# Feed-forward activations split into fp16 pairs two tiles at a time, with eight pair buffers

## The reference

```python
def ffn(x, ...):                                    # 8 experts, top 4 of them, and a shared one
    gate = einsum('bsd,ed->bse', x, Wg) + routing_bias
    weights = softmax over the top 4 of gate
    swiglu = (sigmoid(h) * h * v) @ w3.T            # h = x @ w1.T, v = x @ w2.T, 341 hidden units
    return swiglu_shared(x) + sum_e weights[e] * swiglu_e(x)

x = x + 0.5 * ffn(layernorm(x))
x = x + attention(layernorm(x))                     # 16 heads of 64, causal, softmax
x = x + 0.5 * ffn(layernorm(x))                     # the same weights again
```

## Time and profile before

| | |
|---|---|
| median of 3 runs | 685.14 us (684.83 to 685.91) |
| span of the profiled execution, first to last instruction | 683.0 us |
| TensorE busy | 646.1 us, 95% |
| VectorE busy | 609.6 us, 89% |
| ScalarE busy | 572.8 us, 84% |
| GpSimd busy | 495.7 us, 73% |
| mean granted TensorE clock | 0.995 |

### The profile page before, as it was taken

The page is one execution under the profiler, slowest core; times in us unless marked ns, Lnnn a source line. Parts: engine busy times, 40 slices in busy tenths (PEclk is TensorE's granted clock), DMA queues, the critical chain, the costliest instruction groups (busy, mean ns, idle before and its releaser), DMA issues.

```text
span 683.0 us, 20985 instructions
## 1 busy us (share of the span) xinstructions
PE 646.1 (95%) x7846; PEld 414.1 (61%) x7846; DVE 609.6 (89%) x1701; ACT 572.8 (84%) x1110; POOL 495.7 (73%) x589
## 2 busy tenths in 40 slices
PE   5798989999999998999899999999999999999997
PEld 3465755465567565666566566665666567666665
DVE  4899799999998999899889999989999888789887
ACT  6789977898999888899978999997999997565654
POOL 3244775688899687788967889895789898566555
PEclk9999999999999999999999999999999999999999
DMA  7800000278799366588844788683678797100000
GB/s 205 258 1 1 1 2 1 54 111 148 120 129 154 57 104 120 100 140 123 145 75 79 114 140 141 125 137 56 102 125 134 144 144 110 33 1 18 17 2 16
DMA packets 226489, 62.97 MB, mean 92 GB/s; under 512 B 213202, under 2 KB 225620, under 8 KB 226388
## 3 DMA queue, kind: packets, MB, share of 16 engines
q1 hardware_dynamic: 226388, 61.64, 52.4%
HBM read 7.87 MB, written 1.05 MB: 13 GB/s over the span
## 4 chain that ended last, share of the span: by engine, by line
PE 45%; DVE 23%; ACT 16%; issue 9%; POOL 5%; DMA 1%; SPq 0%; ACTq 0%; DVEq 0%; POOLq 0%
PE bank L1068 13%; PE bank L1070 12%; PE bank L1069 12%; ACT probs L1424 6%; DVE probs L1710 4%; DVE glu L1619 3%; DVE xs L1649 3%; ACT glu L1386 3%; PE bank L1238 3%; DVE glu L1624 3%; POOL paired L1035 2%; ACT gluh L1407 2%; PE bank L1201 2%; POOL glul L1031 1%; ACT paired L1432 1%
## 5 line engine op out<-in xcount | busy, mean ns | idle before, releaser
L1031 POOL TENSOR_TENSOR glul<-glu,gluh 128x512 f16<-128x512 f32 x191 | 221.3, 1161 | 98.4 <-ACT gluh L1407 97.9
L1035 POOL TENSOR_TENSOR paired<-probs,paired 128x512 f16<-128x512 f32 x160 | 185.4, 1161 | 27.4 <-ACT paired L1432 24.5
L1386 ACT ACTIVATE glu<-bank,tanh_scale 128x512 f32<-128x512 f32 x167 | 113.3, 678 | 49.1 <-PE bank L1070 48.5
L1619 DVE SCALAR_TENSOR_TENSOR glu<-glu,bank 128x512 f32<-128x512 f32 x167 | 113.7, 681 | 24.8 <-ACT glu L1386 24.4
L1424 ACT ACTIVATE probs<-probs,exp_bias 128x128 f32<-128x128 f32 (+3 forms) x256 | 131.6, 551 | 3.6 <-POOL exp_bias L1043 3.5
L1710 DVE CUSTOM_DVE_ANT_0 probs<-bank,causal,score_scale 128x128 f32<-128x128 f32 (+3 forms) x256 | 128.0, 545 | 6.2 <-POOL paired L1035 5.0
L1068 PE MATMUL bank<-w3h,gluh 128*128 128x128 f16 x708 | 127.4, 220 | 5.9 <-POOL glul L1031 4.9
L1070 PE MATMUL bank<-w3h,glul 128*128 128x128 f16 x708 | 127.2, 220 | 0.0
L1069 PE MATMUL bank<-w3l,gluh 128*128 128x128 f16 x708 | 127.2, 220 | 0.0
L1407 ACT ACTIVATE gluh<-glu 128x512 f16<-128x512 f32 x191 | 118.5, 621 | 2.0 <-DVE glu L1624 2.0
L1624 DVE SCALAR_TENSOR_TENSOR glu<-glu,bank 128x512 f32<-128x512 f32 x167 | 114.7, 687 | 5.8
(11 more groups left out here) (236 smaller groups left out, 1619.8 us busy)
## 6 DMA issues: line engine op xcount, KB each, us to landing
pT<-paired SPq DMA_TRANSPOSE x160, 3.2
attention_raw<-in_L_attn_W_qkv SPq DMA_DIRECT2D x6, 256.0 KB, 5.3
xs<-in_L_attn_inputs SPq DMA_DIRECT2D x4, 256.0 KB, 4.7
vh<-in_L_ffn_W SPq DMA_DIRECT2D x6, 128.0 KB
pT<-in_L_ffn_W SPq DMA_DIRECT2D x6, 128.0 KB
out<-xs SPq DMA_DIRECT2D x3, 256.0 KB, 2.5
raw_more<-in_L_ffn_W SPq DMA_DIRECT2D x4, 128.0 KB
attention_raw<-in_L_attn_W_out SPq DMA_DIRECT2D x2, 256.0 KB, 6.4
```

The lines of the kernel that those rows point to most:

```text
L1031: pool.tensor_tensor(glul[pair][:, :], g[:, :], gluh[pair][:, :], ALU.subtract).then_inc(glu_low)
L1035: pool.tensor_tensor(paired[n % PAIRED][:, 1, :], probs[n % PROBS][:, :], paired[n % PAIRED][:, 0, :], ALU.subtract).then_inc(probs_low)
L1386: act.activation(g[:, :], psum[b1.bank][:, :], ACT.Tanh, scale=tanh_scale[:, j:j + 1]).then_inc(tanh_made)
L1619: v.scalar_tensor_tensor(g[:, :], g[:, :], 1.0, psum[b1.bank][:, :], ALU.add, ALU.mult).then_inc(drained[b1.bank])
```

## The change

Two neighbouring tiles are split by one instruction of 1024 columns on each engine, every second step. `glu`, `gluh` and `glul` each become one tensor with the buffers side by side, so that two neighbouring buffers can be named by one slice. SPLIT_LAG goes from 2 to 3: at the odd steps i = 3, 5, ... 25 the tiles i - 3 and i - 2 are split together. DOWN_LAG stays 4. GLU_PAIRS goes from 7 to 8, so that a pair of tiles never wraps around. The waits count splits instead of tiles. In stream 7 the tiles 20 and 21 are one split at step 22; tile 22 and the two halves of tile 23 stay as they were. So 191 splits of 512 columns become 95 of 1024 and one of 512.

```diff
-SPLIT_LAG = 2
+SPLIT_LAG = 3
...
-GLU_PAIRS = 7
+GLU_PAIRS = 8
...
-    def split_hidden(self, j, tiles):
-        t = tiles[j]
-        self.add("split_hidden", k=t["k"], g=t["g"], b2=t["b2"], pair=t["pair"], left=self.pair_left[t["pair"]])
+    def split_hidden(self, js, tiles):
+
+        of = [tiles[j] for j in js]
+        first, n = of[0], len(of)
+        assert all(t["g"] == first["g"] + i and t["pair"] == first["pair"] + i for i, t in enumerate(of))
+        self.glu_splits += 1
+        for t in of:
+            t["split"] = self.glu_left[t["g"]] = self.glu_splits
+        self.add("split_hidden", split=self.glu_splits, g=slice(first["g"], first["g"] + n), b2s=[t["b2"] for t in of],
+                 pair=slice(first["pair"], first["pair"] + n), left=max(self.pair_left[t["pair"]] or 0 for t in of))
...
-            elif SPLIT_LAG <= i < HT + SPLIT_LAG:
+                if i < HT:
+                    self.split_hidden({HT - 2: order[HT - 4:HT - 2], HT - 1: order[HT - 2:HT - 1]}[i], tiles)
+            elif SPLIT_LAG <= i < HT + SPLIT_LAG and (i - SPLIT_LAG) % 2 == 0:
                 assert self.scales_known
-                self.split_hidden(order[i - SPLIT_LAG], tiles)
+                self.split_hidden(order[i - SPLIT_LAG:i - SPLIT_LAG + 2], tiles)
...
-                    g, pair = glu[s["g"]], s["pair"]
-                    q.wait_ge(glu_high, s["k"] + 1)
-                    pool.tensor_tensor(glul[pair][:, :], g[:, :], gluh[pair][:, :], ALU.subtract).then_inc(glu_low)
+                    q.wait_ge(glu_high, s["split"])
+                    pool.tensor_tensor(glul_all[:, s["pair"], :], glu_all[:, s["g"], :], gluh_all[:, s["pair"], :],
+                                       ALU.subtract).then_inc(glu_low)
...
-                    q.wait_ge(glu_low, s["k"] + 1)
+                    q.wait_ge(glu_low, s["split"])
                     drain_of(s["w_ready"])
...
-                    b2, pair = s["b2"], s["pair"]
-                    q.wait_ge(drained[b2.bank], b2.n + b2.d)
+                    for b2 in s["b2s"]:
+                        q.wait_ge(drained[b2.bank], b2.n + b2.d)
                     if s["left"]:
                         q.wait_ge(down_done, s["left"])
-                    act.activation(gluh[pair][:, :], glu[s["g"]][:, :], ACT.Copy).then_inc(glu_high)
+                    act.activation(gluh_all[:, s["pair"], :], glu_all[:, s["g"], :], ACT.Copy).then_inc(glu_high)
```

More of the change, by code:

```diff
@@ L323, in hidden @@
         self.glu_taken += 1
-        self.add("hidden", k=k, c=c, j=j, b1=b1, b2=b2, g=g, halves=halves,
+        self.add("hidden", k=k, c=c, j=j, b1=b1, b2=b2, g=g, halves=halves, glu_left=self.glu_left[g],
                  x_ready=self.halves_ready[halves], w_ready=[u for n in OWNERS[j] for u in (self.weights_ready[n, 0], self.weights_ready[n, 1])])
@@ L333, in last_hidden @@
         banks = [(self.bank(), self.bank()) for _ in range(2)]
+        split = self.glu_splits + 1
+        self.glu_splits += 2
         self.add("last_hidden", k=k, c=c, j=j, banks=banks, g=g, halves=halves, x_ready=self.halves_ready[halves],
-                 pair=k % GLU_PAIRS, left=self.pair_left[k % GLU_PAIRS])
-        tiles[j] = {"k": k, "g": g, "b2": banks[1][1], "pair": k % GLU_PAIRS}
+                 pair=k % GLU_PAIRS, left=self.pair_left[k % GLU_PAIRS], glu_left=self.glu_left[g], split=split)
+        tiles[j] = {"k": k, "g": g, "b2": banks[1][1], "pair": k % GLU_PAIRS, "split": split}
     def native_hidden(self, j, tiles):
@@ L357, in down @@
         self.parts += 1
-        self.add("down", part=PARTS.index((j, n)), k=t["k"], pair=t["pair"], first=first, last=last, use=use,
+        self.add("down", part=PARTS.index((j, n)), k=t["k"], split=t["split"], pair=t["pair"], first=first, last=last, use=use,
                  w_ready=self.weights_ready[n, 2])
@@ L378, in down_crossed @@
             first, last = self.turn_of_part(c, n)
-            sides.append({"part": PARTS.index((j, n)), "k": tiles[j]["k"], "pair": tiles[j]["pair"], "first": first,
+            sides.append({"part": PARTS.index((j, n)), "split": tiles[j]["split"], "pair": tiles[j]["pair"], "first": first,
                           "last": last, "use": self.down_uses[n], "w_ready": self.weights_ready[n, 2]})
@@ L756, in macaron @@
         route = [sb(f"route{i}", [P, NE, NT]) for i in range(2)]
-        glu = [sb(f"glu{i}", [P, L]) for i in range(GLUS)]
-        gluh = [sb(f"gluh{i}", [P, L], F16) for i in range(GLU_PAIRS)]
-        glul = [sb(f"glul{i}", [P, L], F16) for i in range(GLU_PAIRS)]
+        glu_all = sb("glu", [P, GLUS, L])
+        gluh_all, glul_all = sb("gluh", [P, GLU_PAIRS, L], F16), sb("glul", [P, GLU_PAIRS, L], F16)
+        glu = [glu_all[:, i, :] for i in range(GLUS)]
+        gluh, glul = ([of[:, i, :] for i in range(GLU_PAIRS)] for of in (gluh_all, glul_all))
         qk = [[sb(f"{n}{i}", [P, L], F16) for n in ("qh", "ql", "kh", "kl")] for i in range(2)]
@@ L1010, in gpsimd @@
                         part = slice(h * L // 2, (h + 1) * L // 2)
-                        q.wait_ge(glu_high, s["k"] + 1 + h)
+                        q.wait_ge(glu_high, s["split"] + h)
                         pool.tensor_tensor(glul[pair][:, part], g[:, part], gluh[pair][:, part], ALU.subtract
@@ L1182, in tensor @@
                         if s["k"] == 2 * B * HT - 1 and t == NT // 2:
-                            q.wait_ge(glu_low, s["k"] + 2)
+                            q.wait_ge(glu_low, s["split"] + 1)
                         done = three_pass(psum[use.bank][:, t * D:(t + 1) * D], gluh[pair][:, rows],
@@ L1191, in tensor @@
                     for side in s["sides"]:
-                        q.wait_ge(glu_low, side["k"] + 1)
+                        q.wait_ge(glu_low, side["split"])
                         drain_of(side["w_ready"])
@@ L1378, in scalar @@
                     q.wait_ge(filled[b1.bank], b1.f + 1)
[L1379 to L1380 removed]
+                    if s["glu_left"]:
+                        q.wait_ge(glu_low, s["glu_left"])
                     q.wait_ge(units_scaled, group_of(OWNERS[j][-1]) + 1 if s["c"] == 0 else len(GROUPS) + 1)
```

8 lines of the change are left out of this document (2 added, 6 removed).

## The result

The changed kernel takes 766.66 us (766.14 to 767.3, 4 runs) against 685.12 us before (684.83 to 685.91, 4 runs): ratio 1.119, 95% interval 1.1175 to 1.1207, 81.5 us more. The forecast was 741.1, range 708 to 772. The span of the profiled execution is 764.8 us, 81.8 us over the one of before.

The account below looks back on a forecast made before the run. TensorE was taken as the bound, waiting for older tiles' low halves. Span 683.0 + 27 (end) + 18 (beside attention) + 10 (start) + 1 (router) = 739.0, with 2.1 outside the span 741.1 us; range 708 to 772.

Parts of the forecast that it names:

- What bounds, and which tile matters: Whole kernel: TensorE sets the pace; its down waits for the low half of a pair's older tile.
- The end stretch: Last 108 us, no attention: low half ready 3.83 us after T, the odd step's tanh start; waits add up, +27 us.
- Beside attention: Middle 445 us: 0.5 us a pair over 54 pairs, less idle time and savings; +18 us, from -11 to +49.
- the recovery: Beside attention: 7 us of new waits fall together with TensorE's present 14 us of idle time, and 2 for the saving.
- Two samples for a mean: Beside attention: two odd steps, one with 0.2 us to spare, one lacking 0.9; 0.5 us taken as mean.
- The start: First 130 us: 18 pairs each 0.8 us short, 14 us, part falling into TensorE's idle time; +10 us, between 2 and 25.
- The router on VectorE: Two VectorE router instructions: longer GpSimd instructions double a shared-port wait, +2.6 us on VectorE, +1 on the path.
- The copy's length: ScalarE's 1024-column copy: 1031 ns from measured sizes; the skill page's 1.15 us would make the sum some 9 us higher.
- (a): Rival, start and beside attention: waits vanish in idle time and shorter queues; 700 us, up to 712; chance 0.09.
- (b): Rival, whole kernel: waits add up in full as at the end; 790 us, everything over 772; chance 0.09 with (d).
- (c): Rival, whole kernel: low half still comes before the down, only savings are left; 680 us; chance 0.03.
- (d): Rival, end stretch: waits lower TensorE's clock to 1.2 GHz, 59 us more, 800 us; chance 0.09 with (b).

Follow-up runs that it names:

- the kernel with two of 512: Changed kernel, but each pair split in the same step by two instructions of 512 columns on ScalarE and two on GpSimd: 712.67 us, ratio 1.039.
- The kernel with more work for TensorE: Changed kernel with the v matmuls of even steps done twice from tile 146 on: 767.14 us, ratio 1.119 to the kernel before.

## Why the prediction was right, and where it was short

- **What bounds, and which tile matters: right.** TensorE waits for the older tile's low half, in every second step. The lead of one step, the length on GpSimd and, at the end, the place behind the tanh each turned out to be needed for the loss: giving back the step (SPLIT_LAG 2), halving the instruction, or taking the copy out from behind the tanh each removes 42 to 64 of the 81.8 us.
- **The end stretch: right in mechanism and nearly in size.** The loop was put at T + 3.83 and is T + 3.90; eight tiles were to lose 4.7 us and lose 21.7 - 16.8 = 4.9, from the 5.43 us of a pair. TensorE's waits there are 25.7 us, about 29 with what the view leaves out of each; forecast 27. The other 4 of the 33.4 were not parted; the lower clock (below) and stream 6's norm and router steps, for which I had 2, are what is left for them.
- **Beside attention: the term that was mis-sized is the recovery.** I took 0.5 us for each of 54 pairs, 27 us. Then I took 9 off, 7 because TensorE's present idle time would absorb some and 2 for the savings. Nothing was absorbed. TensorE's waits for `glul` there rose from 1.9 to 28.1 us, and all its other waits together stayed, 12.2 us before and 12.1 now. The stretch costs 32.8 us; the 6.6 that are left are TensorE shown busy for longer (length, then TensorE's busy time, before and after, tile 36 to tile 144):

```profile
117.00:573.50 456.50, 441.83 (x5789) 280.52 (x5788) 421.51 (x1233) 416.64 (x800) 373.95 (x426) 1.00 0.72 116
132.60:621.80 489.20, 448.02 (x5758) 281.51 (x5757) 425.38 (x1235) 415.14 (x744) 367.15 (x373) 0.99 0.67 109
```

  Of these 6.2 us, 21 more waits of 0.16 us that the view leaves out are 3.4 (an estimate), and the lower clock can be the rest. VectorE's wait for `paired` went from 5.0 to 15.3 us and ScalarE's for `exp_bias` from 3.5 to 11.9. I had named `paired`. But TensorE's other waits did not grow with them, so they are not what the forecast lacked.
- **Two samples for a mean: right by luck.** From two odd steps I read 4.03 and 3.53 us from tanh to down and took 0.5 us for the stretch. Read for all 54 pairs in the trace of before (older tile k: from the tanh of tile k + 3 to the first down matmul behind the v bank of tile k + 4), the distance is below the 3.83 us needed in 27 of them, 0.9 us in the shortest, and the missing time adds up to 26.0 us. The mean is the one I took, but half of the pairs lack nothing and three lack over 2 us.
- **Instructions of 512 at that lag: my largest miss in the experiments.** They cost 28 us where I expected up to 15. The distance is below the 2.44 us they need in only 7 of the 54 pairs, which adds up to 4 us for the even tiles and 9 for all, against 18.9 and 13.2 us lost beside attention. So the distance alone does not explain it. In the kernel with two of 512 the older tile's low half is ready over 2.6 us after T in 23 of the 54 pairs, up to 6.1: the queues of ScalarE and GpSimd make it late, and the sum has no term for that.
- **The start: short by 5.6 us**, forecast 10 and measured 15.6. TensorE's waits for `glul` are 10.9 us against 3.0 before; the rest is TensorE shown busy for 7.7 us longer, with 17.1 of its 37.5 us at the lower clock here. The two were not parted. I had also let its idle time absorb a part: 18 pairs at 0.8 us would have been 14.
- **The router on VectorE: the wait is there, the size is luck.** The two instructions together went up by 3.0 us (forecast 2.6):

```profile
L1600 DVE TENSOR_TENSOR xn<-xn,earlier 128x256 f32<-128x256 f32 x8 | 6.7, 836 | 0.0
L1594 DVE TENSOR_TENSOR xn<-gate 128x256 f32<-128x256 f32 x8 | 5.7, 709 | 0.0
```

  But it was the other one that grew, from 421 to 836 ns, while the one that had been slow stayed so (748, now 709). Each of the 16 taken by itself shows why. Five before and six now begin while a long GpSimd instruction runs, and end 0.28 us after it. All others take 0.40 to 0.43 us; one of these began with such an instruction in its last 0.03 us. The longest pair of now, VectorE and GpSimd:

```profile
683.52 2.07 DVE L1600 TENSOR_TENSOR xn<-xn,earlier 128x256 f32<-128x256 f32 x1
683.18 2.12 POOL L1040 TENSOR_TENSOR glul<-glu,gluh 128x1024 f16<-128x1024 f32 x1 [3.60 <-ACT gluh L1417]
```

  So the wait is for GpSimd's instruction, and which of the two meets one is a matter of where they happen to lie: with the same long subtractions at SPLIT_LAG 2 the 16 take 7.1 us together, less than the 9.4 of before. This agrees with the rule that I had from the Trainium skill ("SBUF — State Buffer", on the shared port pair).
- **The copy's length.** The 0.3 us for an ACTIVATE from the Trainium skill ("ScalarE: Activation LUTs", Rules for kernel authors) is given there for a bias taken from a pointer operand, and the copy has none. It took 1047 ns and not the 1.15 us of that estimate, so the 9 us priced by it did not come.
- **The rivals.** (a) is out: nothing vanished. (b) is out as priced: 49 and 25 us for the first two stretches, measured 32.8 and 15.6, which is nearer the forecast. What holds of it is that the waits are paid in full. (c) is out. (d), the lower clock, was priced for the whole end stretch and given as one thing with (b); it happened in small pieces.

## What to carry to other kernels

Joining two instructions saves their fixed cost, but the first half of the result now arrives with the second; before joining, measure for the first half's reader how long it has, from the last thing that the joined instruction must wait for, and in every place, not in the mean. Where an engine in order feeds the bound engine around a loop, the joined length is paid on every turn, as far as it goes beyond the time that the first half had to spare, and no busy time of the engine shows it. Give back the step of lead together with the merge, or leave the merge out: here the same long instructions cost 82 us with one step to their reader and 17 us with two.

## What was not expected of the hardware

The granted clock of TensorE fell more often in the changed kernel. Of before the trace has two stretches at the lower level, 3.4 us each, inside the program; the changed kernel has ten, 37.5 us together. Busy time by windows in the changed kernel (length, TensorE, weight loads, VectorE, ScalarE, GpSimd, then the granted clock); the first window covers a part of stream 7 with such a stretch, the second one without:

```profile
701.00:707.00 6.00, 4.01 (x23) 2.17 (x22) 3.89 (x9) 2.00 (x3) 2.12 (x1) 0.82 0.14 44
712.00:718.00 6.00, 4.89 (x55) 2.65 (x52) 3.69 (x8) 2.32 (x3) 2.13 (x1) 1.00 0.01 3
```

The pair of steps in the first took 6.53 us from tanh to tanh (700.79 to 707.32) and the pairs behind it 5.42 to 5.53, so this stretch cost 1.1 us. If all eight more of them cost that, the clock has 9 us of the 81.8; this is an estimate, and most likely too high. The kernel with more work for TensorE is the changed one as far as tile 144. It had 6.6 us less at the lower level up to there (24.1 us against 30.7), and reached the tile at 621.5 us against 621.8. In the start alone it had 10.2 us at that level against 17.1, and waited 13.3 us for `glul` against 10.9. So a lower clock makes TensorE busy for longer, and seems to shorten its waits by as much where it waits anyway. TensorE's 21.8 us more of busy time fit two estimates: 30.7 us more at half the clock are at most 15.3 us, and 52 more waits for `glul` of 0.16 us each are 8.3.

The regular waits did not lower the clock by themselves: in stream 7 TensorE waits for ten pairs, and it fell once. Filling the waits with matmuls did not keep it up everywhere either, so what lowers it there is not settled. Nor does it go with the sum of the waits: the changed kernel with DOWN_LAG 5 waits 9.8 us for `glul` and has 31.2 us at the lower level, though I had expected the stretches to go there; the kernel before with SPLIT_LAG 3 waits 30.6 us and has 13.6.
